# First expert stage's early half moved into the last three groups of attention's last batch, in tiles that are dead there

## The reference

```python
x = x + attention(layernorm(x))            # 16 heads of 8, q and k normalised per head, causal softmax
x = x + ffn(layernorm(x))                  # FIRST expert stage
x = x + message(layernorm(x))
x = x + ffn(layernorm(x))                  # second expert stage

def ffn(x):                                # 8 experts, inner width 512
    h = x + layer_norm(x, ln1_g, ln1_b) @ attn_w.T
    t = layer_norm(h, ln2_g, ln2_b)
    logits = t @ gate_w.T                  # top 2 of 8 experts, softmax over the two
    out = sum over e of comb[:, e] * ((silu(t @ gate[e].T) * (t @ up[e].T)) @ down[e].T)
    return h + out
```

## Time and profile before

| | us |
|---|---|
| median of 3 runs | 2870.96 (2869.77 to 2872.42) |
| profiled execution, own time | 2869.91 |
| its span | 2868.2 |
| attention, first to last weighing of scores | 82.4 to 693.2 |
| end of attention's last output add | 701.3 |
| first expert stage: half 0, to its last table row | 702.4 to 734.7 |
| its half 1, to the first block's product | 735.45 to 782.9 |
| busy: PE, DVE, ACT, POOL | 2675.3, 1756.0, 1604.6, 808.9 |

### The profile page before, as it was taken

One profiled execution on the slowest core, in us unless ns is written; L12 is line 12 of the kernel. 1 busy time (PEld: TensorE's weight loads), 2 busy tenths in 40 slices (PEclk: granted clock), 3 DMA queues, 4 the chain that ended last, 5 costly groups with the idle time before them and its releaser, 6 DMA issues. The chain is left out here.

```text
span 2868.2 us, 53413 instructions
## 1 busy us (share of the span) xinstructions
PE 2675.3 (93%) x18798; PEld 1683.4 (59%) x18798; DVE 1756.0 (61%) x3424; ACT 1604.6 (56%) x2677; POOL 808.9 (28%) x1177
## 2 busy tenths in 40 slices
PE   5999998998599889999999999999999999995997
PEld 3555565665488745555555555555555555553886
DVE  7777777775666655555655555555556655555666
ACT  2666666666644455555555556565565555555443
POOL 4142422322456311111111111122121132220652
PEclk8999999999699999999999999999999999998998
DMA  6500000001344268888878887777777788885222
GB/s 108 81 16 16 8 16 16 16 16 52 96 122 147 72 166 193 188 188 194 193 186 188 188 188 185 183 183 178 182 186 184 179 193 200 199 197 199 68 87 86
DMA packets 196571, 383.17 MB, mean 134 GB/s; under 512 B 45281, under 2 KB 108906, under 8 KB 194954
## 3 DMA queue, kind: packets, MB, share of 16 engines
q1 hardware_dynamic: 187722, 362.55, 53.0%
q0 software_dynamic: 8640, 17.84, 1.9%
HBM read 38.10 MB, written 39.86 MB: 27 GB/s over the span
## 5 line engine op out<-in xcount | busy, mean ns | idle before, releaser
L2766 DVE STREAM_TRANSPOSE m_turned<-m_sig 128x1024 f32<-128x1024 f32 x512 | 613.8, 1228 | 480.7 <-ACT m_sig L2536 469.2
L2536 ACT ACTIVATE m_sig<-m_f_ps 128x1024 f32<-128x1024 f32 x512 | 496.5, 1022 | 283.5 <-PE m_f_ps L2368 283.2
L2381 PE MATMUL m_v_ps<-m_sig,m_tok 128*64 128x512 f32 x2048 | 497.4, 607 | 0.0
L2393 PE MATMUL m_v_ps<-m_sigT,m_tok 128*64 128x256 f32 x4064 | 461.1, 380 | 1.4 <-DMA m_sigT<-m_turned 1.4
L1042 DVE TENSOR_REDUCE a_maxima<-a_bank 128x1 f32<-128x512 f32 (+4 forms) x624 | 366.8, 643 | 123.4 <-PE a_bank L637 74.0
L801 ACT ACTIVATE a_prob<-a_bank 128x512 f32<-128x512 f32 (+1 forms) x608 | 321.5, 585 | 191.6 <-PE a_bank L649 188.4
L2368 PE MATMUL m_f_ps<-m_swap,m_own 64*128 64x512 f32 x1536 | 416.4, 404 | 8.0 <-DMA m_swap<-m_own 4.6
L2368 PE MATMUL m_f_ps<-m_own,m_swap 64*128 64x512 f32 x1536 | 416.6, 404 | 0.0
L2393 PEld LDWEIGHTS m_v_ps<-m_sigT,m_tok 128*64 128x64 f32 x4064 | 290.3, 137 | 198.3 <-issue 62.4
L2632 POOL TENSOR_TENSOR m_own<-m_uv,m_own 128x1024 fp32r<-128x1024 f32 x64 | 152.0, 2375 | 731.9 <-ACT m_own L2515 731.9
L2368 PEld LDWEIGHTS m_f_ps<-m_swap,m_own 64*128 64x128 f32 x1536 | 270.1, 186 | 102.3 <-issue 46.9
(11 more groups left out here) (464 smaller groups left out, 4373.0 us busy)
## 6 DMA issues: line engine op xcount, KB each, us to landing
m_sigT<-m_turned SPq DMA_DIRECT2D x2042, 128.0 KB, 2.3
m_swap<-m_own SPq DMA_DIRECT2D x64, 256.0 KB, 3.3
f_t_rows<-f_sent_rows SPq DMA_DIRECT2D x142, 65.0 KB, 2.1
f_sent_rows<-clear_rows SPq DMA_DIRECT2D x34, 260.0 KB, 9.2
k_apart<-a_kT SPq DMA_DIRECT2D x64, 128.0 KB, 2.4
m_swap<-m_own SPq DMA_DIRECT2D x64, 128.0 KB, 3.1
f_h<-back_rows SPq DMA_DIRECT2D x8, 512.0 KB, 5.1
rows<-back_rows SPq DMA_DIRECT2D x6, 512.0 KB, 4.2
```

The lines of the kernel that those rows point to most:

```text
L2381: mm = pe.matmul(v2_ps[h * RANK:(h + 1) * RANK, :], tok[p][:, 0, j + s * SIDE, :], sig[j % 2][s][:, h * HALF:(h + 1) * HALF], start=(j == ...
L2393: mm = pe.matmul(v1_ps[h * RANK:(h + 1) * RANK, g * 2 * P:(g + 1) * 2 * P], tok[p][:, 1, jj, :], sigT[g][:, :, 2 * h:2 * h + 2, jj, :].rea ...
L2536: act.activation(sig[j % 2][s][:, :], f_ps[s][:, :], ACT.Sigmoid).then_inc(sig_ready, 1)
L2766: dve.transpose(turned[g][:, :, q, :, :], sig[j % 2][s][:, :].rearrange("p (t j a) -> p j t a", j=4, a=STACK)).then_inc(turn_ready, 1)
```

## The change

Half 0 of the first expert stage leaves that stage (`moe_phase` loses its `first_half=0` branches: `head(0)`, `choose(0)`, `plain_half`, `count(0)`, `keep_rows(0)`, the 32 sends, the tables) and is written into attention's last batch. `sequence` yields the steps of `early_steps` at the end of a score unit i in groups 1 to 3 of that batch: group 1 has the moments and the head's products in six pieces of three or two tiles; group 2 the second moments, the choice of experts, the counts, the places and 14 sends at i = 23 to 36; group 3 the other 18 sends at i = 0, 2, ... 34. The functions are those of the message stage; they use the same ring of six banks. Tiles: `a_spare` (squares and next values), `a_z` and `a_zT`. `clear_rows` becomes a part of `a_proj`. The phase ends when all 32 sends have landed. The down chunks are now the first work of the expert stage, half 1's roots come right behind them.

```diff
+        STEPS = ((0, 3), (3, 6), (6, 9), (9, 12), (12, 14), (14, 16))
+        SENDS_FROM, SENDS_LATER = 23, 14
...
+        def early_steps(g, i):
+            if g == 1:
+                yield from {0: [("half_moments", 0)], 2: [("half_dev", 0)], 3: [("half_scales", 0)]}.get(i, ())
+                if i in (4, 8, 12, 16):
+                    yield "plain_rows", i // 4 - 1
+                for n in range(len(STEPS)):
+                    at = 5 * n + 5
+                    if i in (at, at + 2, at + 5):
+                        yield {at: "head_rows", at + 2: "head_turn", at + 5: "head_product"}[i], n
+            elif g == 2:
+                if i in (1, 4, 7, 10):
+                    yield "add_rows", i // 3
+                yield from {0: [("second_moments", 0)], 2: [("second_dev", 0)], 3: [("second_scales", 0)], 5: [("route_first", 0)],
+                            8: [("route_second", 0)], 10: [("count", 0)], 12: [("route_blocks", 0)], 15: [("route_firsts", 0)],
+                            18: [("route_places", 0)], 21: [("early_table", 0)]}.get(i, ())
+                if 4 <= i < 4 + 2 * EARLY // 2 and i % 2 == 0:
+                    yield "keep_rows", i // 2 - 2
+                if SENDS_FROM <= i < SENDS_FROM + SENDS_LATER:
+                    yield "send", i - SENDS_FROM
+            elif i % 2 == 0 and SENDS_LATER + i // 2 < EARLY_SENDS:
+                yield "send", SENDS_LATER + i // 2
...
+                if prev and not prep:
+                    yield from early_steps(g, i)
...
+            def head_rows(i):
+                act.wait_ge(half_scaled, 1)
+                for j, t in enumerate(range(*STEPS[i])):
+                    ins = act.activation(head_norm[:, j * DIM:(j + 1) * DIM], k["x"][:, t * DIM:(t + 1) * DIM], ACT.Identity, ...)
+            def keep_rows(i):
+                act.wait_ge(early_summed, i // 2 + 1)
+                act.wait_ge(second_scaled, 1)
+                for t in range(2 * i, 2 * i + 2):
+                    ins = act.activation(early[:, t, 0:DIM], early[:, t, 0:DIM], ACT.Identity, bias=away2[:, t:t + 1], scale=rstd2[:, t:t + 1])
...
+            def send(j):
+                t, choice = divmod(j, TOP)
+                pool.wait_ge(places_ready, 1)
+                pool.wait_ge(rows_kept, t // 2 + 1)
+                pool.indirect_dma_start(k["sent_rows", "f1"][:, :], ..., early[:, t, :], None).then_inc(k["sent", "f1"][0], 16)
...
+            pool.wait_ge(k["sent", "f1"][0], 16 * EARLY_SENDS)
...
+            def head_sums(u, i):
+                u.wait_full(dve)
+                dve.wait_ge(plain_done, (t1 - 1) // GTOK + 1)
+                dve.tensor_tensor(own, own, product[:, :, 0:DIM], ALU.add).then_inc(head_taken, 1)
+                dve.tensor_copy(raw_logits[:, t0:t1, :], product[:, :, DIM:]).then_inc(u.free(), 1)
+                for t in range(t0, t1):
+                    ins = dve.bn_stats(flat_stats[:, t * 6:(t + 1) * 6], early[:, t, 0:DIM])
...
-            if not first_half:
-                head(0)
-                keep_rows(0)
             if first_time:
                 for c in range(DOWNS):
                     weight_high(c)
-            act.wait_ge(var_ready, 2 - first_half)
+            act.wait_ge(var_ready, 1)
             half_deviations(act, k, 1).then_inc(dev_ready, 1)
             head(1)
...
-                plain_half()
-                pool.wait_ge(places_ready, 1)
-                pool.wait_ge(norm_kept, HALF_GROUPS)
-                for j in range(SENT):
-                    send(0, j)
```

More of the change, by code:

```diff
@@ L686, in project_out, with head_turn, head_product, count @@
                 mm.then_inc(unit_full, 1)
+            def head_turn(u, i):
+                pe.wait_ge(head_normed, i + 1)
+                return turn_tiles(u, lambda t: head_norm[:, (t - STEPS[i][0]) * DIM:(t - STEPS[i][0] + 1) * DIM], range(*STEPS[i]))
+            def head_product(u, i, turned):
+                out = u.next()
+                u.wait_empty(pe, turned)
+                for j in range(STEPS[i][1] - STEPS[i][0]):
+                    mm = pe.matmul(out[:, j * HEAD_COLS:(j + 1) * HEAD_COLS], head_normT[:, j * P:(j + 1) * P], k["head_w"][:, :],
+                                   start=True, stop=True)
+                mm.then_inc(unit_full, 1)
+            def count(u):
+                out = u.next()
+                u.wait_empty(pe)
+                pe.wait_ge(chosen_ready, 1)
+                flat = chosen.rearrange("p t e -> p (t e)")
+                pe.matmul(out[:, 0:ROUTE], k["below"][:, :], flat, start=True, stop=True)
+                pe.matmul(out[:, ROUTE:2 * ROUTE], k["ones"][:, :], flat, start=True, stop=True)
+                pe.matmul(out[:, 2 * ROUTE:2 * ROUTE + P], k["ones"][:, :], k["below"][:, :], start=True, stop=True).then_inc(unit_full, 1)
             def group(u, b, g, prev, prep, follows, shifted, high=None):
@@ L936, in group @@
                         stack_queries(b + 1 if g in (2, 3) else b, n)
+                    elif what == "plain_rows":
+                        plain_rows(n)
+                    elif what == "add_rows":
+                        add_rows(n)
+                    elif what == "send":
+                        send(n)
                 return projects
@@ new lines, in route_second, with take_counts @@
+            def route_second(link):
+                pick_first(link, other, second[:, 0:EARLY], first_at)
+                dve.tensor_tensor(chosen, pick, other, ALU.add).then_inc(chosen_ready, 1)
+            def take_counts(u):
+                src = u.next()
+                u.wait_full(dve)
+                for i, to in enumerate((earlier_rows, tile_counts)):
+                    dve.tensor_copy(to, src[:, i * ROUTE:(i + 1) * ROUTE].rearrange("p (t e) -> p t e", e=EXPERTS))
+                dve.tensor_copy(k["numbers"][:, :], src[:, 2 * ROUTE:2 * ROUTE + NB]).then_inc(u.free(), 1)
+                u.wait_emptied(dve, u.n)
@@ new lines, in route_places @@
+            def route_places(link):
+                dve.scalar_tensor_tensor(out=place, in0=over_tiles(firsts[:, 0, :]), scalar=float(P), in1=place, op0=ALU.mult, op1=ALU.add)
+                link(dve.tensor_tensor(beyond, beyond, over_tiles(jump), ALU.mult))
+                link(dve.scalar_tensor_tensor(out=place, in0=beyond, scalar=float(P), in1=place, op0=ALU.mult, op1=ALU.add))
+                for i, one in enumerate((pick, other)):
+                    ins = dve.tensor_tensor(places_of[i], one, place, ALU.mult)
+                link(ins)
+                for i in range(TOP):
+                    ins = dve.tensor_reduce(row_of32[:, i, :], places_of[i], AX.X, ALU.add)
+                link(ins)
+                dve.tensor_copy(k["early_rows"][:, :, :], row_of32[:, :, :]).then_inc(places_ready, 1)
```

339 lines of the change are left out of this document (234 added, 105 removed).

## The result

| | before | after |
|---|---|---|
| median of 4 runs, us | 2870.55 (2869.77 to 2872.42) | 2893.12 (2889.23 to 2893.82) |
| ratio | | 1.0075, 95% interval 1.0057 to 1.0092 |
| profiled execution: span | 2868.2 | 2891.9 |

The change is slower by 22.6 us; 2885 was forecast, in a range of 2871 to 2896.

The account below looks back on a forecast made before the run. TensorE was taken to bound groups 1 and 2, and a chain through half 0 the expert stage's opening. 11.1 + 10.6 + 11.9 - 19.2 = +14.4 us on 2869.9 gave 2884.3, forecast as 2885, range 2871 to 2896.

Parts of the forecast that it names:

- the stretches: Sign in attention's last batch: group stretches of about 46, 45 and 32 us against 35.6, 34.0 and 20.2.
- The waits for GpSimd: Sign in group 3: TensorE waits some 10 us for GpSimd's select.
- the queue without gaps: Sign in groups 2 and 3: GpSimd shows no gaps from the first send to the last keep.
- Sends, 11.9 forecast: Groups 2 and 3: GpSimd's queue of 32 sends and twelve keeps, 49.5 us, becomes the bound; 11.9 us, ends 9 and 17.
- Group 2, 10.6 forecast: Group 2: VectorE's 16.4 us of routing, less its idle time and TensorE's lead, cost 10.6 us; ends 4.7 and 16.4.
- The first part and group 1, 11.1 forecast: Group 1 and its start: TensorE matrix work 6.7, VectorE pieces 2, moments and scales 2.4; sum 11.1 us.
- The matrix work and the pieces, 6.7 + 2: Group 1: products and transposes cost TensorE 6.7 us at full price; VectorE's six head pieces cost 2, ends 0 and 8.
- The 2.4 for "moments and scales": Group 1's start: VectorE's moments and scales and two ScalarE table loads, taken at half of 4.7; ends 0 and 4.7.
- The opening, 19.2 forecast: Expert stage's opening: half 1 starts at 716.2 instead of 735.45, 19.2 us gained; 21 or 16 depending on loads.
- stops cost the clock too: Rival: lower clock after TensorE's stops, or loads delaying half 1, add some 8 us; 2893, chance 0.10.
- the idle time of VectorE and GpSimd takes everything: Rival, from group 2's i = 23 and its routing: idle time absorbs the work; -5.4 us, 2865.6, chance 0.10.
- The contention: Skill rule, group 2: VectorE and GpSimd contend in SBUF, up to four waits of about 1 us; left out of sum.

Follow-up runs that it names:

- sends_in_stage: The change with all 32 sends issued by GpSimd at the expert stage's opening, from a tile kept alive past attention; 2880.29 us, 1.0035 of the kernel before.
- routing_in_group3: sends_in_stage with all of group 2's early steps moved at the same i to group 3; 2870.73 us, 1.0005 of the kernel before.
- fitted_to_idle_time: sends_in_stage with early steps moved to idle places: later moments and head pieces, picks, counts and places in group 3; 2863.59 us, 0.9982 of the kernel before.
- detours_clock_kept: before_two_detours with TensorE repeating the unit ahead of each of its two stops; 2881.49 us, 1.0033 of the kernel before.
- moments_three_later: The change with the half's moments, roots and scales at i = 3, 4, 5 of group 1 instead of 0, 2, 3; 2892.88 us.
- before_two_detours: The kernel before with useless chained VectorE products in the last batch, nine in group 1 and 24 in group 2; 2883.96 us, 1.0049 of it.
- roots_asked_later: fitted_to_idle_time with moments at i = 5, root 9, scales 11, pieces from 14; on another chip 2929.55 us, 0.9991 of the kernel before.

## Why the prediction was right, and where it was low

The direction held, each of the four terms is found in the runs, and the result lies in the range, but only 3 us under its upper end. All four terms missed to the same side: measured in the runs, 13.8 + 15.0 + 12.8 - 17.7 = 23.9 stands for the 14.4 of the sum, 9.5 us more. The order of the three costs came out reversed: sends were forecast as the largest and are the smallest, group 2 is the largest. The forecast by place was rougher than the sum. The first part is 5.9 longer, not 2; the stretches are 48.4, 50.6 and 27.2, not 46, 45 and 32, since part of the queue's delay already falls before group 3's output copy. The waits for GpSimd, 10.0, and the queue without gaps came as said.

- **Sends, 11.9 forecast.** 12.8 by sends_in_stage, and the queue's 49.5 us were 50.3. Right. The rest, 0.9 us, is within what two medians can tell; in the traces after's last two stretches are 12.3 longer.
- **Group 2, 10.6 forecast.** sends_in_stage against routing_in_group3 in its second stretch (3.8), and against before in its third (45.3 - 34.1 = 11.2): 15.0 us, near the end of 16.4 that the prediction gave as the plain price. The term was mis-sized in its first number: 16.4 us of VectorE were taken at 0.29 us an operation. Six operations from 646.94 to 658.18 that take 0.17 or 0.29 elsewhere took 0.55 to 1.15, 3.8 us more in all, each beside one of GpSimd's four adds or a keep and ending within 0.2 us of its end. With 20.2 instead of 16.4, the prediction's own subtraction gives 20.2 - 3.3 - 2.5 = 14.4. No run takes the adds alone away from the chain, so this share is worked out and not measured. Nothing in the term stood for the low clock behind each stop either (a mean of 0.85 in the third stretch of sends_in_stage).
- **The first part and group 1, 11.1 forecast.** 13.8. The matrix work and the pieces, 6.7 + 2, were priced about right. Most of them lie in the second stretch, 7.9 longer, and in the first two windows of fitted_to_idle_time TensorE is busy 38.9 + 42.8 us, 8.7 over the earlier trace rows, at a clock of 0.98. The 2.4 for "moments and scales" was mis-sized: 5.9 in the first stretch, where the head has only its first three transposes beside them: a stop of 3.0 us, for the casts, and a clock of 0.50 from 602 to 610 behind it:

```profile
602.00:606.00 4.00, 3.59 (x22) 1.91 (x23) 1.56 (x4) 3.99 (x9) 2.34 (x4) 0.50 0.00 0
606.00:610.00 4.00, 4.00 (x18) 3.62 (x17) 1.39 (x3) 3.76 (x8) 3.92 (x6) 0.50 0.01 4
```

The nearest row had given 4.7; "I take half" had no row behind it.
- **The opening, 19.2 forecast.** 17.7. From the stage's first load to half 1 it is 758.63 - 745.13 = 13.5 us, forecast as 716.2 - 702.4 = 13.8. The miss lies ahead of it, in a tail that was taken as unchanged; TensorE there after, then before:

```profile
735.20 1.97 PE L662 MATMUL a_bank<-ident,a_oT 128*128 128x128 f32 x8 [1.12 <-ACT a_oT L897]
737.09 1.94 PE L662 MATMUL a_bank<-ident,a_o_tok 128*128 128x128 f32 x8
738.94 3.07 PE L749 MATMUL a_bank<-w_o,a_o_tokT 128*128 128x128 f32 x16
```

```profile
694.37 1.09 PE L598 MATMUL a_bank<-ident,a_oT 128*128 128x128 f32 x8 [1.12 <-ACT a_oT L806]
695.79 1.11 PE L598 MATMUL a_bank<-ident,a_o_tok 128*128 128x128 f32 x8 [0.33 <-DVE a_o_tok L1062]
697.19 2.02 PE L685 MATMUL a_bank<-w_o,a_o_tokT 128*128 128x128 f32 x16 [0.28 <-ACT a_o_tokT L795]
```

TensorE enters the tail at 0.50, and the way from the output copy to the stage's first load is 1.9 us longer. About half of that goes with the sends. The other 0.9 stays in sends_in_stage, where group 3's waits are those of before: the clock falls at the tail's start there too (0.59 from 722 to 726), and why is open. In fitted_to_idle_time, whose tail is as long as before, 19.8 came back.

The rival "stops cost the clock too" gave 2893, and the result is 2893.1. That match is partly luck, since its 8 us were a round figure. Its mechanism is real, but detours_clock_kept puts it at a third of one detour's price; VectorE's operations that last longer beside GpSimd's are another part. How the 8 us divide stays open. The rival by which the idle time of VectorE and GpSimd takes everything was wrong for this order of steps, and nearly right for another: in fitted_to_idle_time, with the sends in the stage, the last two stretches cost nothing, and the result, 2863.6, lies near its 2865.6.

Of the rules weighed ahead: no drain shows here either, 604.28 + 1.28 = 605.56 and the exponential starts at 605.58, against the Trainium skill (ScalarE: Activation LUTs, What ACT_TABLE_LOAD costs). By the Trainium skill (SBUF — State Buffer, Who interferes with whom) VectorE operations with two SBUF inputs contend with GpSimd reading SBUF; the traces agree, with 1.15 and 0.83 for 0.29, and 0.51 for 0.35 in the detours. Two of the six slow operations have one input, though (647.52 above is one of them), so this rule alone doesn't cover all of them. The contention was left out of the sum and belonged in it.

## What to carry to other kernels

An engine's idle time is worth what the stretch leaves at that moment, not on average. The group 2 steps cost 15 us in a group in which VectorE had its maxima. All of them moved as they were to the next, where it has none, they cost 9 us in the one trace there is (by the medians about 5). Cut up, with picks, counts and places there and moments, adds and row writes left in group 2, they cost next to nothing: all four stretches are then 13.9 us over before, and the head alone had cost 13.8. Before a chain is laid beside a full engine, look at each consumer of the chain on that engine's queue: a unit that asks too early stops everything behind it, and the work after the stop runs slower for a while. And a queue that waits for nobody else (GpSimd in the stage's opening) is the place for 40 us of descriptors, if the tile they read can be kept alive.

## What was not expected of the hardware

- A VectorE operation of 0.29 us took up to 1.15 while GpSimd ran its 128x512 additions (1.2 us each), four times its time, and ended when the addition did.
- In after, moments_three_later and before_two_detours stops of 3.0 to 5.5 us were followed by 4 us or more at a clock of 0.50; one of 2.35 us (roots_asked_later) was not, but one of 1.8 us (detours_clock_kept) was followed by some 3 us of it. The length of the stop alone doesn't decide.
- On one chip the kernel before took 2.2% longer (2933.05 against 2869.5); the wait of 24.2 us above is the one place of it that was looked at.
